# Who adds the two halves of the softmax sums: VectorE in place of GpSimd in a global attention stage

## The reference

```python
q = (x @ Wq)        # 16 heads of 64
k, v = (x @ Wkv)    # 4 key heads, 4 value heads of 64
q, k = q * cos + rotate_half(q) * sin, k * cos + rotate_half(k) * sin
attn = softmax(q @ k.T / 8, over 2048 keys)
out = (attn @ v) @ Wo + bo
```

## Time and profile before

| | us |
|---|---|
| median of 3 runs | 3734.76 |
| lowest, highest | 3733.58, 3739.41 |
| the profiled execution's own time | 3737.75 |
| its span | 3736.0 |
| mean granted TensorE clock, share of full speed | 0.943 |

### The profile page before, as it was taken

How to read it: one execution, slowest core, us unless ns; L and a number is a source line. 1 busy time by engine, 2 the same in 40 slices (tenths; PEclk the granted TensorE clock), 3 DMA queues, 4 the chain that set the end, 5 groups by cost and what they waited for, 6 DMA issues and landing times. The chain is left out here.

```text
span 3736.0 us, 70352 instructions
## 1 busy us (share of the span) xinstructions
PE 3254.7 (87%) x27870; PEld 1992.5 (53%) x27870; DVE 2669.1 (71%) x4726; ACT 1946.8 (52%) x3456; POOL 1687.1 (45%) x1133
## 2 busy tenths in 40 slices
PE   5999999999747368998699999999999999969997
PEld 3667777777636256777333333333333333337776
DVE  4667667676655857777677777787778777667776
ACT  2445444444423219999344444444444444439997
POOL 0121212121114226665166666666666666756664
PEclk8999999999968669999799999999999999979999
DMA  2000000000010010000100000000000000010000
GB/s 95 2 1 2 2 2 1 2 2 2 2 54 2 6 55 1 2 2 2 30 1 1 1 1 1 1 1 1 1 1 1 1 1 1 1 46 2 2 2 13
DMA packets 22482, 31.76 MB, mean 8 GB/s; under 512 B 8610, under 2 KB 18252, under 8 KB 20940
## 3 DMA queue, kind: packets, MB, share of 16 engines
q1 hardware_dynamic: 22156, 27.26, 2.2%
HBM read 26.20 MB, written 1.05 MB: 7 GB/s over the span
## 5 line engine op out<-in xcount | busy, mean ns | idle before, releaser
L3190 POOL TENSOR_TENSOR global_acc_pool<-global_acc_pool,global_probs 128x1024 f32<-128x1024 f32 x320 | 796.6, 2489 | 246.3 <-ACT global_probs L3131 222.3
L3131 ACT ACTIVATE global_probs<-global_ps 128x1024 f32<-128x1024 f32 x512 | 519.9, 1024 | 626.6 <-PE global_ps L2986 611.2
L3257 DVE TENSOR_REDUCE global_part<-global_ps 128x2 f32<-128x1024 f32 x512 | 622.7, 1218 | 304.3 <-PE global_ps L2968 304.1
L2986 PE MATMUL global_ps<-global_q,global_k 64*128 64x512 f32 x2048 | 529.8, 595 | 0.0
L2997 PE MATMUL global_ps<-global_probs,global_v 128*64 128x512 f32 x2048 | 495.7, 605 | 0.0
L970 POOL TENSOR_TENSOR delta_etm<-delta_et,C_tile 128x1024 f32<-128x1024 f32 x16 | 40.2, 2514 | 755.6 <-ACT delta_et L853 755.6
L2968 PE MATMUL global_ps<-global_khh,global_qhh 64*128 64x512 f32 x1024 | 307.1, 597 | 59.0 <-DVE global_part L3257 52.0
L2984 PE MATMUL global_ps<-global_mrow,global_first 64*128 64x512 f32 x1024 | 321.1, 624 | 0.0
L2968 PEld LDWEIGHTS global_ps<-global_khh,global_qhh 64*128 64x128 f32 x1024 | 97.2, 187 | 375.9 <-DVE global_part L3257 300.5
L2997 PEld LDWEIGHTS global_ps<-global_probs,global_v 128*64 128x64 f32 x2048 | 124.2, 136 | 266.0 <-issue 178.2
L1071 DVE COPY_PREDICATED delta_Yd<-delta_tri,delta_ps 64x512 f32<-64x512 uint32 x160 | 116.6, 729 | 191.3 <-PE delta_ps L587 188.8
(11 more groups left out here) (584 smaller groups left out, 7090.5 us busy)
## 6 DMA issues: line engine op xcount, KB each, us to landing
delta_cw<-in_conv_taps SPq DMA_DIRECT2D x4, 1024.0 KB, 10.6
local_tab<-in_rot_tables SPq DMA_DIRECT2D x2, 2048.0 KB, 12.4
local_tab<-in_rot_tables SPq DMA_DIRECT2D x2, 1536.0 KB, 7.7
localw_wqkv<-in_L_ffn_wqkv SPq DMA_DIRECT2D x2, 768.0 KB
delta_wqkvz<-in_L_attn_a_W_qkvz SPq DMA_DIRECT2D x1, 1024.0 KB, 5.6
local_tab<-in_rot_tables SPq DMA_DIRECT2D x2, 512.0 KB, 4.2
global_cos<-in_rope_cos SPq DMA_DIRECT2D x8, 128.0 KB, 3.3
global_sin<-in_rope_sin SPq DMA_DIRECT2D x8, 128.0 KB, 3.3
```

The source lines that it names most:

```text
L2986: mm = pe.matmul(ps[:, 2 * (at % 2) + s, :], k2[own, group_of(u) % 2, P * k:P * k + P], q[own, u % 3, :], start=False, stop=True)
L3131: act.activation(probs[:, at % RING, :], ps[:, 2 * (at % 2):2 * (at % 2) + 2, :].rearrange("p b n -> p (b n)"), ACT.Exp).then_inc(S["probs ...
L3190: ins = eng.tensor_tensor(sums[:, u % 2, :], sums[:, u % 2, :], probs[:, at % RING, :], ALU.add)
L3257: dve.tensor_reduce(part[:, u % 2, r % SLOTS, :], ps[:, rough_banks(r), :], X_AXIS, ALU.max)\
```

## The change

The merge of the two engines' sums moves from GpSimd to VectorE, where it stands in span 1 of the next unit between the maximum and `join_rotated`. It writes its result to `acc` in place of `acc_pool`, and the out_sums matmul reads `acc`. The last unit's merge stands behind VectorE's last addition. The waits of the merge are the same two as before. No DMA is added, removed or moved.

```diff
@@ out_sums on TensorE
-                    mm = pe.matmul(ps[own, 7, :], ones[:, 0:HD], acc_pool[:, u % 2, BLK * s:BLK * s + BLK],
+                    mm = pe.matmul(ps[own, 7, :], ones[:, 0:HD], acc[:, u % 2, BLK * s:BLK * s + BLK],
@@ GpSimd
-                def merge_sums(u):
-                    pool.wait_ge(S["sum_step"], (u + 1) * len(dve_adds))
-                    pool.wait_ge(S["odd_step"], (u + 1) * (TILES - len(dve_adds)))
-                    pool.tensor_tensor(acc_pool[:, u % 2, :], acc_pool[:, u % 2, :], acc[:, u % 2, :], ALU.add)\
-                        .then_inc(S["merged"], 1)
@@ GpSimd's loop over the tiles
-                    if at % TILES == 1 and at >= TILES:
-                        merge_sums(at // TILES - 1)
                     if at % TILES == 7 and at >= TILES:
                         normalize_context(at // TILES - 1)
-                merge_sums(UNITS - 1)
                 normalize_context(UNITS - 1)
@@ VectorE
+                def merge_sums(u):
+                    dve.wait_ge(S["sum_step"], (u + 1) * len(dve_adds))
+                    dve.wait_ge(S["odd_step"], (u + 1) * (TILES - len(dve_adds)))
+                    dve.tensor_tensor(acc[:, u % 2, :], acc[:, u % 2, :], acc_pool[:, u % 2, :], ALU.add)\
+                        .then_inc(S["merged"], 1)
@@ VectorE's loop over the spans, behind the span's first part_max
+                        if j == 1 and u:
+                            merge_sums(u - 1)
                         if j == 1 and u + 2 < UNITS:
                             join_rotated(("q", u + 2))
@@ VectorE, after the loop
                 adds_of(TILES * UNITS - 1)
+                merge_sums(UNITS - 1)
                 invert_sums(UNITS - 1)
```

## The result

| | before | after |
|---|---|---|
| median, us (6 runs each) | 3736.91 | 3750.62 |
| lowest to highest | 3733.58 to 3739.45 | 3748.47 to 3753.62 |
| span of the profiled execution | 3736.0 | 3749.8 |

The changed kernel takes 1.0038 of the time before, 95% interval 1.0025 to 1.005: 13.7 us slower. (Three more runs beside the changed kernel moved the median before from 3734.76 to 3736.91.) The forecast was 3751 with 3739 to 3766 around it. The stage itself, from its first projection on TensorE (1804.47 us before, 1803.08 after) to its last addition to X (3302.53 and 3313.76), grew from 1498.1 to 1510.7 us, by 12.6; the other 1.2 us of the span lie in stages that the change does not touch.

The account below looks back on a forecast made before the run. TensorE's pace plus short waits for VectorE was taken to bound the stage. 25 x 0.51 + 4 x 1.2 - 1.2 = +16.4 us took the profiled 3737.75 to 3754.1; the median forecast was 3751 us, range 3739 to 3766.

Parts of the forecast that it names:

- Bottleneck: Global attention stage: TensorE's pace plus short waits for VectorE's maxima sets the time; GpSimd's merge is off the path until the end.
- D: Rival: the faster engine saves 2.36 - 1.21 us per merge, -37 us in all, 3698 us; chance 0.01.
- Price of the merge: VectorE, span 1: merge +2.15 us, join -1.25, so the second row maximum starts 0.90 us later.
- order of turns: VectorE and GpSimd two-operand work alternates by whole instructions, first asker first; GpSimd's tile 2 delays the merge to about 2.2 us.
- A: Rival: VectorE's merge goes unhindered by GpSimd's tile 2, -14 us, 3721 us; chance 0.06, its no-change middle case 0.08.
- B: Rival: GpSimd's tile 2 passes VectorE's waiting add, first maximum 2.35 us late, +51 us, 3786 us; chance 0.05.
- second wait: TensorE's second wait in a unit for a VectorE maximum, before the rough scores: 0.30 us becomes 1.20.
- Given back: VectorE's copy of tile 3 meets fewer GpSimd additions, 1.1 us in place of 1.74; 0.39 us per unit recovered.
- third wait: TensorE's third wait in a unit for a VectorE maximum, 0.44 us before the change, forecast near 0.
- Special units: Four units with GpSimd quiet at VectorE's tile 15: GpSimd's tile 2 goes first and delays it, +1.2 us each.
- rival C: Half of 29 new TensorE waits bring a clock drop, +22 us on top, 3773 us; chance 0.08.
- The end: The last unit's merge is on the path before out_sums: 2.34 us becomes 1.14, -1.2 us.

Follow-up runs that it names:

- E1: Changed kernel with one wait more: GpSimd adds tile 2 only when VectorE's merge is done; 0.9986 of the time of the kernel before.
- E4: Changed kernel with the merge left out on every engine, so the denominators hold VectorE's tiles only; 0.9951 of the time of the kernel before.
- E7: The changed kernel once more, unaltered, on another chip; 1.0039 of the time of the kernel before.
- E6: Kernel before the change, with the merge still on GpSimd but behind tile 2 in place of tile 1; 0.9986 of the time of the kernel before.

## Why the prediction was right

The forecast added 16.4 us and the change cost 13.7. That 3751 and 3750.62 lie closer than that is partly luck: three more runs raised the median before by 2.15 us. The mechanism and the price per regular unit held; the term for the four special units, those in which GpSimd is quiet when VectorE adds tile 15, came out too large.

**Bottleneck.** Right. Nothing on GpSimd's side mattered but its turns; out_sums waited for the merge once in 32, as before, 1.2 us in place of 2.4. D, the engine's speed, had the sign wrong.

**Price of the merge, +0.90 at the second maximum.** Measured +0.92: merge 2.24, join 0.68. The order of turns was the step that could have failed (A and B), and it held: the merge takes 1.2 only in three units and in the last two merges. E1 shows that without the turn the same 1.2 us of work make no loss against the kernel before: the second wait is 0.19, under the 0.30 of before.

The Trainium skill (SBUF — State Buffer, "Who interferes with whom") says that a VectorE instruction with two SBUF inputs contends with a GpSimd instruction that reads SBUF, and that the port pair which they share is an exclusive lock. This case agrees: the merge takes 2.24 behind GpSimd's tile 2 and 1.21 where GpSimd is made to wait (E1).

**Given back, 0.39 per unit.** Right in kind: the third wait is gone, and E1 against E4 shows it coming and going with the copy. The copy alone was guessed at 1.1 us and takes 0.68; that changed nothing, because the maximum behind it waits for TensorE. Net per regular unit +0.51 forecast, +0.54 to 0.57 measured.

**Special units, 4 x 1.2.** This was the mis-sized term, with the mechanism as told: GpSimd's tile 2 starts first and VectorE's tile 15 pays. TensorE and VectorE after, in one such unit:

```profile
2740.19 0.50 PE L2968 MATMUL global_ps<-global_khh,global_qhh 64*128 64x512 f32 x2 [1.28 <-DVE global_part L3248]
2743.59 0.50 PE L2968 MATMUL global_ps<-global_khh,global_qhh 64*128 64x512 f32 x2 [1.04 <-DVE global_part L3248]
2746.46 0.49 PE L2968 MATMUL global_ps<-global_khh,global_qhh 64*128 64x512 f32 x2 [0.19 <-DVE global_part L3248]
```

```profile
2740.06 2.35 DVE L3190 TENSOR_TENSOR global_acc<-global_acc,global_probs 128x1024 f32<-128x1024 f32 x1
...
2743.46 1.21 DVE L3288 TENSOR_TENSOR global_acc<-global_acc,global_acc_pool 128x1024 f32<-128x1024 f32 x1
```

There are three of them after (11, 19 and 20) and four before (3, 11, 19 and 21). Each follows a unit in which the clock fell, which the prediction held fixed; units 1 to 30 have six falls in the trace before, four in the one after. E7, the same kernel as the changed one, has four falls and four special units, so the lower count can't be credited to the change. Beyond the regular length of its kind a special unit takes 1.5 to 2.2 us before, 1.7 in the mean, and 1.6 to 2.2 after, 1.9 in the mean (1.9 in E7 too). One thus costs 0.2 us over the regular rate, in place of the 1.2 - 0.5 = 0.7 forecast.

With +0.54 in each of 29 units, units 1 to 30 would be 15.7 longer; they are 13.6 longer. The term was forecast at 4 x 0.7 = +2.8 over the regular rate; together with the falls that did not happen it came out at -2. That is more than the distance between the 17.6 us forecast without the end and the 13.6 measured in these units; the regular units' 0.03 more each works the other way.

**Clock, rival C.** Not so. The new waits of 1.2 us brought no fall in units without keys; windows of the kernel after (busy us by engine, then granted clock), beside the earlier trace rows:

```profile
2540.00:2585.00 45.00, 43.28 (x219) 17.83 (x217) 34.32 (x34) 19.76 (x22) 27.30 (x13) 1.00 0.00 1
2720.00:2765.00 45.00, 40.60 (x191) 15.79 (x187) 36.47 (x33) 19.62 (x23) 26.10 (x12) 0.96 0.00 1
```

Each of the ten falls in units 1 to 30 of the two traces starts within 1.7 us after the end of one of TensorE's 1.7 us waits for the mask row (L2953). None starts elsewhere, not even after the wait of 1.62 us for a maximum in unit 20 after. A fall is a stretch of 3.4 us at 1.2 GHz; one of the kernel before:

```profile
2359.00:2362.40 3.40, 3.40 (x10) 1.17 (x8) 1.75 (x2) 2.15 (x4) 0.00 (x0) 0.50 0.00 0
```

The 4% of 45 us that the prediction read is the share of full speed that is lost, 1.7 us; the time at the lower level is twice that.

The Trainium skill's section on psum-queue depth-cycling (TensorE: Matmul & The Clock Gate) tells of small idles between groups of matmuls, frequent enough to swing the clock. Waits of 1.2 us once per unit did not do so: the granted clock stays at 1.00, the upper level of 2.4 GHz, there.

**The end.** out_sums waits 1.24 in place of 2.39: -1.15 for -1.2.

## What to carry to other kernels

Before moving work to a faster engine, find the instruction on that engine whose result the bottleneck waits for, and count the queue ahead of it: here the same merge costs 1.1, 0.6 or 0.15 us per regular unit, and its place decides more than its engine. Two-operand work of VectorE and GpSimd takes turns by whole instructions, so taking a job off GpSimd lets its next one start earlier, just ahead of what was put on VectorE. A wait added to the engine that has time can be a gain (E1, 0.9986 against 1.0038). And look at the irregular units too: E6 won 0.4 us per unit and lost some two thirds of that in five units.

## What was not expected of the hardware

A copy of 128x1024 on VectorE from SBUF to SBUF takes 0.68 us alone, little more than half of an addition of that size (1.21), but mostly 1.5 to 2.1 beside GpSimd's additions; like an addition it waits for its turn, though it has one operand. E1 and E4 show both sides on one chip. The Trainium skill (SBUF — State Buffer, "Who interferes with whom") counts copies in a two-port mode among what takes the shared ports. The two durations agree with that, but no row shows the mode itself.
